# A cross-attention and gated-FFN layer: a pair's full-array products gathered in two of its four macros, half of the output projection one pair later, and VectorE's order changed with them

## The chip, the cores and the metric

The kernel runs on one core of one Trainium2 chip. The metric is device time in microseconds (us) of one execution. TensorE (PE) does the matrix products, VectorE (DVE) and ScalarE (ACT) the elementwise work, GpSimd (POOL) splits tiles and weights into high and low parts, and SyncE (SP) issues nearly all DMAs.

## The reference, cut to what matters

```python
B, Q, S, D, HEADS, DH = 4, 512, 1024, 256, 16, 64
lat = layer_norm(layernorm(x), g, b);  ctx = layer_norm(ctx_1024, g, b)
q = heads(lat @ Wq);  k, v = heads(split(ctx @ Wkv))
k = rope(k, cos, sin)
attn = softmax(clip(q @ k.T / 8, -11, 11));  x = x + (attn @ v) @ Wo + bo
t = layernorm(x)                               # then 16 experts, hidden 128, D 256
x = x + sum_e(relu(t @ keys[e]) * sigmoid(t @ sel[e])) @ values[e])
```

The clip is applied after the exponential, by its limits e^-11 and e^11, which is the same. All large products except attn @ v take operands that are split in a high and a low part and are the sum of three products (high·high, high·low, low·high).

## The kernel before, in words

The attention works on 32 pairs (4 batches of 8 pairs of heads, 128 columns). Each engine has a function `iteration(n)` that emits its work on pair n in an order written out by hand; nothing is scheduled by a tool, and engines meet only in semaphores. A pair has 8 steps of 128 context rows, two to a macro, so four macros m = 0 to 3.

On PE a macro is three blocks:

- **scores**: `scores(n, s)` for two steps, q times k of two heads in the two halves of the array's rows (in the trace `64*128`, source line L846);
- **full-array products** (`128*128`, L147 from the helper `product`): what the next pairs need;
- **attend**: `attend(n, s)` for the two steps of the macro before, probabilities times v of two heads in the two halves of the array's columns (`128*64`, L859). Macro 0 attends the last two steps of pair n-1 and ends with `denominators(n - 1)` (`128*32`, L872), the column sums of the summed probabilities.

The full-array products of pair n are, before the change: in macro 0 k of pair p = n+1 (`project_k`, two halves, into job_ps0 and job_ps1); in macro 1 q of pair p (`q_product`, job_ps0), the first half of v for a later pair (`project_v(n, 0)`, job_ps1), and the first half of the output projection of pair n-2 (`project_y(..., mt=0)`, into side_ps); in macro 2 the transposes of one context tile (`turn_tile`, pairs 0 to 21; every second one, with x rows, has four instead of two) and the second half of the output projection; in macro 3 the second half of v (job_ps0, after `q_split`). Pairs 30 and 31 have no v to make.

ACT does `exp` of two steps per macro, rounds q and k to their high parts (`round_q`, `round_k`), copies k, v, the attended output and the denominators out of PSUM (`evac_k`, `store_v`, `evac_o`), and applies the layer norm's affine part to a turned tile. DVE does per pair: `clip` of eight steps, four `sum_up` (two steps' probabilities added), two `sum_quad` (denominators wait for both), `rope_times` (two products), `rope_add`, `split_q`, `split_k`, two `add_y`, `scale_o`, `split_o`, `invert_den`, and `stats` and `normalize` of a tile. POOL computes the tile's reciprocal deviation (`rstd`), splits it (`split_tile`), and in pairs 0 to 5 also splits weights (`split_weights`, `split_v_weights`).

SP's queue per pair, in this order: four DMAs of `swap_k(p)` (rows of k swapped for the rope, after `evac_k`), the next context tile, `turn_den(n-1)`, `store_inv(n-1)`, `spread_inv(n-1)`, and from pair 5 on `fetch_pack(n+3)`, two DMAs of 384 KB with split weights, which wait until both halves of the output projection of pair n-2 are done (the pack's buffer holds that pair's Wo).

Buffers that order the work: two score banks, so `scores(n, s)` waits for `exp` of step s-2; four probability buffers, so `exp` of step s waits for `attend` and `sum_up` of step s-4; job_ps0 and job_ps1 for k, q, v and tiles; side_ps for both halves of the output projection and the denominators, each after the last reader's `add_y` or copy. `evac_o(n-1)` waits for `split_o(n-2)`.

## Time and profile before

| | us |
|---|---|
| median of 3 runs (1039.69 to 1040.93) | 1039.74 |
| the profiled execution, its own time | 1040.09 |
| its span, first to last instruction | 1037.9 |
| PE busy | 987.5 (95%) |
| DVE busy | 821.8 (79%) |
| ACT busy | 514.9 (50%) |
| POOL busy | 256.5 (25%) |

The attention runs from about 49 to 837 us of the span, the experts after it. In the attention PE executes almost without a gap. A busy PE is not a PE at its peak: the start of each matmul matters, since matmuls overlap in the pipeline, so the rows below are to be read by the distance from one start to the next.

### The profile page before, as it was taken

What the parts mean: (1) busy time and instruction counts of PE and PEld (TensorE: products, weight loads), DVE (VectorE), ACT (ScalarE), POOL (GpSimd) and SP (SyncE); (2) the same over time, 40 slices, a digit from 0 to 9 for tenths busy, and PEclk for the clock granted to TensorE, in tenths of its full rate; (3) what the DMA queues carried; (4) which work ended last, traced back from release to release, by engine and by line L of the source; (5) the groups of instructions that cost most, each with busy time, mean ns of one, the idle gap of its engine ahead of it and who ended that gap; (6) DMA issues with size and microseconds to landing.
All of it is one profiled execution on the core that took longest, in us unless ns stands there. A gap on an engine that the chain in (4) does not pass through costs nothing. (4 is left out here: it accounts for less than half of the span.)

```text
span 1037.9 us, 15273 instructions
## 1 busy us (share of the span) xinstructions
PE 987.5 (95%) x5336; PEld 605.9 (58%) x5336; DVE 821.8 (79%) x1239; ACT 514.9 (50%) x759; POOL 256.5 (25%) x241
## 2 busy tenths in 40 slices
PE   4599999999999999999999999999999889999998
PEld 3455555555555555555555555555555358888886
DVE  5499999888989999999999978998889876545422
ACT  5465555555555555655555555555555442222221
POOL 5442423211111111211111100321000135545442
PEclk9799999999999999999999999999999899999999
DMA  6344333332323232322222233222222471332321
GB/s 172 114 143 126 100 93 106 100 93 68 92 67 93 71 102 89 97 87 73 87 72 88 71 93 83 82 82 82 82 62 64 130 256 53 122 123 101 123 82 41
DMA packets 68952, 100.34 MB, mean 97 GB/s; under 512 B 21968, under 2 KB 44752, under 8 KB 66832
## 3 DMA queue, kind: packets, MB, share of 16 engines
q1 hardware_dynamic: 68880, 99.41, 31.7%
q8 instruction: 41, 0.67, 0.3%
q14 instruction: 31, 0.25, 0.1%
HBM read 70.01 MB, written 10.75 MB: 78 GB/s over the span
## 5 line engine op out<-in xcount | busy, mean ns | idle before, releaser
L1033 ACT ACTIVATE wide_a<-score_ps 128x1024 f32<-128x1024 f32 x256 | 249.2, 1029 | 149.1 <-PE score_ps L846 149.1
L1239 DVE TENSOR_SCALAR wide_a<-wide_a 128x1024 f32<-128x1024 f32 x256 | 181.5, 740 | 74.9 <-ACT wide_a L1033 74.8
L1248 DVE TENSOR_TENSOR p_sum<-wide_a 128x1024 f32<-128x1024 f32 x128 | 161.7, 1263 | 2.3
L859 PE MATMUL o_ps<-wide_a,values_a 128*64 128x512 f32 x512 | 124.0, 605 | 0.0
L859 PE MATMUL o_ps<-wide_a,v_sb 128*64 128x512 f32 x512 | 124.0, 605 | 0.0
L846 PE MATMUL score_ps<-q_hi,k_hi 64*128 64x512 f32 x512 | 115.6, 448 | 0.8 <-DVE k_lo L1218 0.8
L1781 DVE SCALAR_TENSOR_TENSOR act<-h_ps,wide_a 128x512 f32<-128x512 f32 x64 | 44.2, 690 | 90.0 <-PE h_ps L147 88.2
L846 PEld LDWEIGHTS score_ps<-q_hi,k_hi 64*128 64x128 f32 x512 | 48.4, 185 | 111.9 <-issue 99.6
L1552 POOL TENSOR_TENSOR act_lo<-act,act_hi 128x512 fp32r<-128x512 f32 x64 | 84.8, 1324 | 96.5 <-ACT act_hi L1698 96.5
L1698 ACT CAST act_hi<-act 128x512 fp32r<-128x512 f32 x64 | 39.7, 621 | 135.4 <-DVE act L1781 135.4
L846 PE MATMUL score_ps<-q_hi,k_lo 64*128 64x512 f32 x512 | 102.0, 394 | 0.0
L846 PE MATMUL score_ps<-q_lo,k_hi 64*128 64x512 f32 x512 | 101.8, 393 | 0.0
L649 POOL CAST wide_hi<-ctx_t 128x256 fp32r<-128x256 f32 x22 | 23.9, 1088 | 241.3 <-ACT x_t L986 123.2
L1254 DVE TENSOR_TENSOR p_sum<-p_sum 128x1024 f32<-128x1024 f32 x64 | 78.3, 1224 | 0.0
L634 POOL TENSOR_TENSOR rstd_sb<-var_sb,power 128x2 f32<-128x2 f32 x32 | 30.7, 958 | 180.6 <-DVE var_sb L1172 101.2
L1040 ACT COPY o_raw<-o_ps 128x512 f32<-128x512 f32 x32 | 18.8, 587 | 107.1 <-DVE o_lo L211 105.8
L147 PE MATMUL job_ps<-wv_hi,wide_hi 128*128 128x256 f32 x240 | 70.8, 295 | 0.0
L147 PE MATMUL job_ps<-wv_hi,wide_lo 128*128 128x256 f32 x240 | 67.7, 282 | 0.0
L147 PE MATMUL job_ps<-wv_lo,wide_hi 128*128 128x256 f32 x240 | 67.5, 281 | 0.0
L859 PEld LDWEIGHTS o_ps<-wide_a,v_sb 128*64 128x64 f32 x512 | 31.0, 136 | 57.4 <-issue 47.9
L859 PEld LDWEIGHTS o_ps<-wide_a,values_a 128*64 128x64 f32 x512 | 31.0, 136 | 55.3 <-issue 45.8
L147 PE MATMUL job_ps<-wide_hi,w_hi 128*128 128x512 f32 x128 | 55.2, 431 | 5.1 <-POOL wide_lo L639 2.8
(203 smaller groups left out, 2006.5 us busy)
## 6 DMA issues: line engine op xcount, KB each, us to landing
wide_a<-sel_dram SPq DMA_DIRECT2D x16, 1024.0 KB, 4.6
k_swap<-k SPq DMA_DIRECT2D x124, 128.0 KB, 2.3
w_hi<-packs_hi SPq DMA_DIRECT2D x26, 384.0 KB, 3.9
w_lo<-packs_lo SPq DMA_DIRECT2D x26, 384.0 KB, 4.4
den<-inv_dram SPq DMA_DIRECT2D x64, 128.0 KB, 2.9
ctx_raw<-ctx SPq DMA_DIRECT2D x24, 128.0 KB, 2.3
packs_hi<-w_hi SPq DMA_DIRECT2D x8, 384.0 KB, 3.3
packs_lo<-w_lo SPq DMA_DIRECT2D x8, 384.0 KB, 3.6
```

What stands on the lines that cost most here:

```text
L147: mm = pe.matmul(out, lhsT, rhs, start=start and i == 0, stop=stop and i == len(terms) - 1)
L634: pool.tensor_tensor(rstd_sb[slot][:], var_sb[slot][:], power[:], ALU.pow).then_inc(rstd_ready, 1)
L649: pool.tensor_copy(ctx_at(ctxT_hi, t), ctx_t32[:]).then_inc(tile_hi, 1)
L846: mm = pe.matmul(score_ps[s % 2][:, h, :], k[par][rows, s * P:(s + 1) * P], q[par][rows, :], start=(i == 0), stop=(i == len(terms) - 1))
L859: mm = pe.matmul(o_ps[DH * h:DH * h + DH, :], v_sb[n // 2 % 2][:, at:at + DH], probs[s % RING][:, h, :], start=(s == 0), stop=(s == STEPS ...
L1033: act.activation(probs[s % RING][:], score_ps[s % 2][:], ACT.Exp, scale=DH ** -0.5).then_inc(exp_done, 1)
L1239: dve.tensor_scalar(probs[s % RING][:], probs[s % RING][:], CLIP_HI, CLIP_LO, ALU.min, ALU.max).then_inc(clipped, 1)
L1248: dve.tensor_tensor(p_sum[m][:], first, second, ALU.add).then_inc(summed_up, 1)
L1254: dve.tensor_tensor(second[:], first[:], second[:], ALU.add).then_inc(quads_up, 1)
L1552: pool.tensor_tensor(act_lo[e % ARING][:], act32[e % ARING][:], act_hi[e % ARING][:], ALU.subtract).then_inc(act_split, 1)
L1698: act.copy(act_hi[e % ARING][:], act32[e % ARING][:]).then_inc(act_hi_done, 1)
L1781: dve.scalar_tensor_tensor(out=act32[e % ARING][:], in0=h_ps[e % ARING][:], scalar=0.0, in1=gates[:, at:at + 512], op0=ALU.max, op1=ALU.mu ...
```

## The change

PE's full-array products of macros 1 and 3 go to macro 2, and the second half of the output projection goes one pair on, to macro 0. Macros 1 and 3 are then scores and attend alone (in the last pair the second half for pair 29 stays in macro 3). The order of DVE and ACT follows.

```diff
 # PE
                     scores(n, 2 * m)
                     scores(n, 2 * m + 1)
+                    if m == 0 and n >= 3:
+                        pe.wait_ge(y_added, 2 * (n - 3) + 1)
+                        project_y(pe, sh, n - 3, 1, side_ps, w_hi[n % 2], w_lo[n % 2], (n - 1) % 2)
                     if m == 0 and p < NPAIR:
                         project_k(p, 0)
                         project_k(p, 1)
-                    if m == 1 and p < NPAIR:
+                    if m == 2 and p < NPAIR:
                         pe.wait_ge(k_evac, 2 * p + 1)
                         q_product(p)
-                    if m == 1 and n + 2 < NPAIR:
+                    if m == 2 and n + 2 < NPAIR:
                         project_v(n, 0)
+                    if m == 2 and n >= 2:
+                        pe.wait_ge(den_evac, n)
+                        pack_ready(n - 2 + WO_LAG)
+                        project_y(pe, sh, n - 2, 0, side_ps, w_hi[p % 2], w_lo[p % 2], n % 2)
+                    if m == 2 and n + 2 < NPAIR:
+                        project_v(n, 1)
                     if m == 2 and t < TILES:
...
-                    if m == 3 and n + 2 < NPAIR:
-                        project_v(n, 1)
-                    if n >= 2 and m in (1, 2):
...
+                    if m == 3 and n == NPAIR - 1:
+                        pe.wait_ge(y_added, 2 * (n - 2) + 1)
+                        project_y(pe, sh, n - 2, 1, side_ps, w_hi[p % 2], w_lo[p % 2], n % 2)
 # ACT
-                    if m == 1:
+                    if m == 2:
                         if p < NPAIR:
                             round_q(p)
                         if n + 2 < NPAIR:
                             store_v(j, FILLS + 2 * n)
-                    if m == 2:
                         if p < NPAIR:
                             round_k(p)
+                        if n + 2 < NPAIR:
+                            store_v(j, FILLS + 2 * n + 1)
...
                     if m == 3:
-                        if n + 2 < NPAIR:
-                            store_v(j, FILLS + 2 * n + 1)
 # DVE
                 for m in range(MACROS):
-                    if m == 2 and p < NPAIR:
-                        rope_add(p)
-                    if m == 3 and n >= 2:
+                    last = n == NPAIR - 1
+                    if m == 1 and t < TILES:
+                        dve.wait_ge(turned, t)
+                        normalize(t, ctx_n[:], x_n[:])
+                    if last and m == 3:
                         add_y(dve, sh, n - 2, 1, side_ps, bo)
...
+                    if m == 1 and p < NPAIR:
+                        rope_times(p)
                     clip(n, 2 * m + 1)
-                    if m == 1 and p < NPAIR:
-                        split_q(p)
                     if m == 0 and n > 0:
                         sum_quad(n - 1, 1)
+                    if m == 0 and n >= 3:
+                        add_y(dve, sh, n - 3, 1, side_ps, bo)
+                    if m == 2 and n >= 2:
+                        add_y(dve, sh, n - 2, 0, side_ps, bo)
                     sum_up(n, m)
...
                     if m == 1:
...
                         if n > 0:
                             invert_den(dve, sh, n - 1)
...
                         if p < NPAIR:
-                            rope_times(p)
+                            split_q(p)
+                            rope_add(p)
                     if m == 2:
...
                             split_k(p)
...
                         if n > 0 and not last:
                             scale_o(dve, sh, n - 1)
                         if not last:
                             sum_quad(n, 0)
```

On PE, around macro 3 of a middle pair: before, the twelve v products, of which the last five are shown, stand between the scores and attend.

```order
L147 MATMUL job_ps<-wv_lo,wide_hi 128x256
L147 MATMUL job_ps<-wv_hi,wide_lo 128x256
L147 MATMUL job_ps<-wv_hi,wide_hi 128x256
L147 MATMUL job_ps<-wv_lo,wide_hi 128x256
L147 MATMUL job_ps<-wv_hi,wide_lo 128x256
L859 MATMUL o_ps<-wide_a,v_sb 64x512 x4
```

After, macro 3's scores are followed by attend, then by the scores of the next pair's macro 0, then by the second half of the output projection (side_ps) and the first products of k (wide_hi, w_hi).

```order
L846 MATMUL score_ps<-q_lo,k_hi 128x512 x2
L859 MATMUL o_ps<-wide_a,v_sb 64x512 x4
L846 MATMUL score_ps<-q_hi,k_hi 128x512 x2
L846 MATMUL score_ps<-q_hi,k_lo 128x512 x2
L846 MATMUL score_ps<-q_lo,k_hi 128x512 x2
L846 MATMUL score_ps<-q_hi,k_hi 128x512 x2
L846 MATMUL score_ps<-q_hi,k_lo 128x512 x2
L846 MATMUL score_ps<-q_lo,k_hi 128x512 x2
L147 MATMUL side_ps<-o_hi,w_hi 128x512
L147 MATMUL side_ps<-o_lo,w_hi 128x512
L147 MATMUL side_ps<-o_hi,w_lo 128x512
L147 MATMUL job_ps<-wide_hi,w_hi 128x512
```

The scores and attend of macros 1 and 3 now touch, and the v products stand in macro 2.

On DVE, macro 1 of a pair without x rows, before: both clips (wide_a), `split_q` (q_lo), `sum_up`, `normalize` (ctx_n), `invert_den`, `add_y`, `rope_times` (k, k_swap), then `rope_add`.

```order
L1239 TENSOR_SCALAR wide_a<-wide_a 128x1024 x2
L1202 TENSOR_TENSOR q_lo<-job_ps,q_hi 128x512
L1248 TENSOR_TENSOR p_sum<-wide_a 128x1024
L1182 TENSOR_SCALAR ctx_n<-ctx_raw,mv_c,rstd_sb 128x256
L175 TENSOR_TENSOR inv_rows<-den_rows 128x8
L177 RECIPROCAL inv_rows<-inv_rows 128x8
L223 TENSOR_TENSOR yT<-side_ps,yT 128x512
L1208 TENSOR_TENSOR k<-k,cos_sb 128x1024
L1209 TENSOR_TENSOR k_swap<-k_swap,sin_sb 128x1024
L1213 TENSOR_TENSOR k<-k,k_swap 128x1024
```

After, the same macro, to the first clips of macro 2:

```order
L1184 TENSOR_SCALAR ctx_n<-ctx_raw,mv_c,rstd_sb 128x256
L1241 TENSOR_SCALAR wide_a<-wide_a 128x1024
L1210 TENSOR_TENSOR k<-k,cos_sb 128x1024
L1211 TENSOR_TENSOR k_swap<-k_swap,sin_sb 128x1024
L1241 TENSOR_SCALAR wide_a<-wide_a 128x1024
L1250 TENSOR_TENSOR p_sum<-wide_a 128x1024
L175 TENSOR_TENSOR inv_rows<-den_rows 128x8
L177 RECIPROCAL inv_rows<-inv_rows 128x8
L1204 TENSOR_TENSOR q_lo<-job_ps,q_hi 128x512
L1215 TENSOR_TENSOR k<-k,k_swap 128x1024
L1241 TENSOR_SCALAR wide_a<-wide_a 128x1024 x2
```

`normalize` has moved ahead of the clips and the rope's products between them; `split_q` has moved behind `invert_den`, where it waits for the q product of PE's macro 2.

## Rows read from the trace of the kernel before

**Rows 1.** Busy time by stage: us, PE, PEld, DVE, ACT, POOL, PEclk, DMA share, GB/s
```profile
49.00:809.00 760.00, 749.86 (x4255) 422.45 (x4256) 677.95 (x939) 426.22 (x598) 138.22 (x127) 1.00 0.31 90
```

**Rows 2.** Timeline of PE, pair 14 from macro 1's products on: start, length, work
```profile
402.58 0.50 PE L147 MATMUL job_ps<-xT_hi,w_hi 128*128 128x512 f32 x1
...
406.30 1.94 PE L859 MATMUL o_ps<-wide_a,v_sb 128*64 128x512 f32 x8
408.16 0.50 PE L846 MATMUL score_ps<-q_hi,k_hi 64*128 64x512 f32 x2
...
414.18 0.39 PE L846 MATMUL score_ps<-q_lo,k_hi 64*128 64x512 f32 x2
414.50 0.39 PE L147 MATMUL job_ps<-wv_hi,wide_hi 128*128 128x256 f32 x1
414.72 0.28 PE L147 MATMUL job_ps<-wv_lo,wide_hi 128*128 128x256 f32 x1
...
416.11 1.94 PE L859 MATMUL o_ps<-wide_a,v_sb 128*64 128x512 f32 x8
417.97 0.50 PE L846 MATMUL score_ps<-q_hi,k_hi 64*128 64x512 f32 x2
```

**Rows 3.** Timeline of PE, macro 3 of pair 30, which has no full-array product
```profile
806.40 0.39 PE L846 MATMUL score_ps<-q_lo,k_hi 64*128 64x512 f32 x2
806.72 1.94 PE L859 MATMUL o_ps<-wide_a,v_sb 128*64 128x512 f32 x8
```

**Rows 4.** Timeline of PE, the denominators of pairs 0, 5, 16, 17, 29, 30 and 31
```profile
78.38 1.07 PE L872 MATMUL side_ps<-p_sum,ones 128*32 128x512 f32 x8 [0.75 <-DVE p_sum L1254]
...
203.74 1.06 PE L872 MATMUL side_ps<-p_sum,ones 128*32 128x512 f32 x8
...
473.57 1.06 PE L872 MATMUL side_ps<-p_sum,ones 128*32 128x512 f32 x8
...
497.78 1.06 PE L872 MATMUL side_ps<-p_sum,ones 128*32 128x512 f32 x8
...
794.03 1.06 PE L872 MATMUL side_ps<-p_sum,ones 128*32 128x512 f32 x8
...
815.96 1.93 PE L872 MATMUL side_ps<-p_sum,ones 128*32 128x512 f32 x8 [3.60 <-DVE p_sum L1254]
...
836.59 1.06 PE L872 MATMUL side_ps<-p_sum,ones 128*32 128x512 f32 x8 [1.44 <-DVE p_sum L1254]
```

**Rows 5.** Timeline of ACT, macros 1 and 2 of the pair of rows 2
```profile
405.27 0.62 ACT L1012 CAST q_hi<-job_ps 128x512 fp32r<-128x512 f32 x1
...
409.17 1.94 ACT L1033 ACTIVATE wide_a<-score_ps 128x1024 f32<-128x1024 f32 x2 [2.78 <-PE score_ps L846]
```

**Rows 6.** Timeline of DVE, the same pair
```profile
406.06 0.68 DVE L1202 TENSOR_TENSOR q_lo<-job_ps,q_hi 128x512 fp32r<-128x512 f32 x1
...
409.32 1.22 DVE L1208 TENSOR_TENSOR k<-k,cos_sb 128x1024 f32<-128x1024 f32 x1
410.45 1.22 DVE L1209 TENSOR_TENSOR k_swap<-k_swap,sin_sb 128x1024 f32<-128x1024 f32 x1
...
412.85 1.29 DVE L1239 TENSOR_SCALAR wide_a<-wide_a 128x1024 f32<-128x1024 f32 x2
...
417.05 1.82 DVE L1239 TENSOR_SCALAR wide_a<-wide_a 128x1024 f32<-128x1024 f32 x2
```

**Rows 7.** Timeline of DVE, `normalize` in pair 0
```profile
60.16 1.91 DVE L1182 TENSOR_SCALAR ctx_n<-ctx_raw,mv_c,rstd_sb 128x256 f32<-128x256 f32 x1
```

**Rows 8.** Timeline of POOL, `split_weights` in pair 0
```profile
59.24 2.68 POOL L670 TENSOR_TENSOR w_lo<-w_raw,w_hi 128x768 fp32r<-128x768 f32 x1
```

**Rows 9.** Timeline of SP's queue, four issues of `swap_k`
```profile
423.27 2.46 SPq L516 DMA_DIRECT2D k_swap<-k  x4
```

**Rows 10.** The page, DMA issues: count, KB each, median us to landing
```profile
k_swap<-k SPq DMA_DIRECT2D x124, 128.0 KB, 2.3
w_lo<-packs_lo SPq DMA_DIRECT2D x26, 384.0 KB, 4.4
```

More of the change, by code:

```diff
@@ L947, in iteration @@
                             logits(pe, sh, job_ps[1], lambda k: xT_hi[:, 0, k, :], lambda k: xT_lo[:, 0, k, :])
-                    if m == 3 and n + 2 < NPAIR:
-                        project_v(n, 1)
-                    if n >= 2 and m in (1, 2):
-                        if m == 1:
-                            pe.wait_ge(den_evac, n)
-                            pack_ready(n - 2 + WO_LAG)
-                        else:
-                            pe.wait_ge(y_added, 2 * (n - 2) + 1)
-                        project_y(pe, sh, n - 2, m - 1, side_ps, w_hi[p % 2], w_lo[p % 2], n % 2)
+                    if m == 3 and n == NPAIR - 1:
+                        pe.wait_ge(y_added, 2 * (n - 2) + 1)
+                        project_y(pe, sh, n - 2, 1, side_ps, w_hi[p % 2], w_lo[p % 2], n % 2)
                     if m > 0:
@@ L1112, in iteration @@
                             evac_o(n - 1)
-                    if m == 1:
+                    if m == 2:
                         if p < NPAIR:
@@ L1325, in iteration @@
                 for m in range(MACROS):
-                    if m == 2 and p < NPAIR:
-                        rope_add(p)
-                    if m == 3 and n >= 2:
+                    last = n == NPAIR - 1
[3 more added lines that the diff above has]
+                    if last and m == 3:
                         add_y(dve, sh, n - 2, 1, side_ps, bo)
-                    last = n == NPAIR - 1
-                    if last and m == 3:
                         split_keys(3)
@@ L1349, in iteration @@
                     if m == 1:
-                        if t < TILES:
-                            dve.wait_ge(turned, t)
-                            normalize(t, ctx_n[:], x_n[:])
                         if n > 0:
                             invert_den(dve, sh, n - 1)
-                        if n >= 2:
-                            add_y(dve, sh, n - 2, 0, side_ps, bo)
                         if p < NPAIR:
-                            rope_times(p)
+                            split_q(p)
+                            rope_add(p)
                     if m == 2:
@@ L1363, in iteration @@
                             split_k(p)
-                        if n == 29:
-                            invert_gate(dve, sh, 0, 1)
-                    if m == 3:
                         if n > 0 and not last:
@@ L1370, in iteration @@
                             sum_quad(n, 0)
+                        if n == 29:
+                            invert_gate(dve, sh, 0, 1)
+                    if m == 3:
                         if n == 23:
```

## The prediction, made before the changed kernel had run

> **What bounds the kernel now.** I read the stage table first. From 49 to 809 us of the span PE is busy for 749.9 of 760 us at the full clock, 2.4 GHz; DVE is busy for 678 us, 89%, so it is the second bound and its order matters [rows 1]. Then the timeline of PE, by starts. Attend runs eight passes in 408.16 - 406.30 = 1.86 us, so a slot of 512 columns takes 0.2325 us [rows 2]. The full-array products of macro 1 are nine slots of 512 and twelve of half that, 15 slots or 3.49 us, and take 3.72; those of macro 3 are six slots' worth, 1.395 us, and take 416.11 - 414.50 = 1.61 [rows 2]. So a visit to the full array costs 0.23 and 0.21 us beside its work. One can see where: the first product's slot is 0.22 in place of 0.116 (414.50 to 414.72), the rest is in the last slot before attend. Entering from the scores costs 0.32 - 0.23 = 0.09 (414.18 to 414.50), but scores that go straight to attend pay the same 0.32 [rows 2, 3], so that part stays.
>
> Third, the starts of the denominators, one per pair. Pair 17's is 24.21 us after pair 16's, a pair in which PE waits for nothing [rows 4]. The 24 pairs to number 29 take 794.03 - 203.74 = 590.3 us against 24 x 24.21 = 581.0; some 4 us of the 9.3 are transposes and logits that pair 17 has not (estimated from the slots), so 5 us are waits. The five to number 5 take 125.4 against 5 x 24.21 - 1.4 (pair 1 has no output projection, six slots) = 119.7: over 5 us are waits. Pair 0 has about 2 more. At the end come 3.60 and 1.44 us of waiting for `sum_quad`, and after the first of them PE runs at its lower level, 1.2 GHz: the same denominators take 1.93 instead of 1.06 [rows 4].
>
> **The change, part by part.**
>
> *Two visits less per pair.* No product is added or removed. Macros 1 and 3 lose their visit, 0.21 + 0.23 = 0.44 us, which I take as 0.42 since v's second half and the moved y product may keep a few hundredths where they join. The moved work falls into visits that exist. Pairs 0 to 29 gain this, 12.6 us; pair 30 gains one visit, and pair 31 has one more (the product for pair 28 in macro 0). Sum: -12.5 us. A direct look at a pair whose macros 1 and 3 are bare exists only at the end [rows 3].
>
> The Trainium skill, "TensorEngine Tiling (Array Packing)", Key Properties, says that changing the tiling mode drains TensorE. By that rule each change of form costs, scores to attend as well. Counting changes, a pair has 13 before and 11 after; the rows put 0.09 at the end of the scores whichever form follows, and more at both ends of a full-array visit, so the sum goes by the visit.
>
> *DVE's new chain to `split_q`.* This is the one place where PE newly waits in the middle of its work: `project_v(n, 1)` waits for `q_split` in the same macro, with tile transposes and attend queued behind it. From macro 2's start PE wants it after scores 1.6, q 1.5, v 1.4, y 0.7 = 5.2 us. The q product ends at 1.6 + 1.5 + 0.2; the cast is 0.62 [rows 5] and `split_q` 0.68 [rows 6], so it is ready at 4.6: a margin of 0.6 us, if DVE is free at 3.9. DVE's chain there starts with the exp of macro 1. The exps end 1.0 and 1.0 us apart, the first about 2.0 us after the scores' start (409.17 is 1.0 after 408.16, the pair of them 1.94) [rows 2, 5], or 2.3 if ACT first has to copy the output of the last pair. Then come clip 0.6, two rope products 2.3, clip 0.6, a sum 1.15 and the inverses 0.3: 4.95 [rows 6]. That is 7.0 to 7.3 after macro 1's start. Macro 1 is now 1.6 + 1.86 = 3.46 long, so DVE is free 3.5 to 3.8 us into macro 2, just before q's high part is there. In a middle pair PE loses nothing; behind this DVE has work until `sum_quad`, which now ends about 4.7 us into macro 0, against 7.1 where the denominators want it (scores 1.6, y 0.7, k 3.0, attend 1.86). So the waits of the middle pairs go, and those for head rows too, since `sum_up` of macro 3 no longer has `scale_o` and a `sum_quad` between it and them. Of the 5 us I leave 1.3 for pairs with x rows, where POOL's splits lengthen DVE's clips (1.82 in place of 1.29) [rows 6]: -3.7 us.
>
> *Pairs 0 to 5.* Here POOL splits weights just while DVE is in that chain. In pair 0 `normalize` took 1.91 us and ended at 62.07, right after POOL's 2.68 us split that ended at 61.92 [rows 7, 8]. Before, this lay in macro 1 with the whole pair to make it good. Now one such block (some 1.5 us) is 0.9 more than the margin of 0.6, so 0.9 us in pairs 1, 3, 4 and 5, and about 2.5 in pairs 0 and 2, where v weights are split as well: 8.6 us. They take the place of 7.3 us of waits: +1.3 us. The bounds: if POOL's splits fall beside ACT-bound moments, 3 us of waits remain (-4); if each is met twice, 12 (+5). The value is nearest to the one block that the row shows.
>
> The Trainium skill, "SBUF — State Buffer", "Who interferes with whom", says the pair of ports that DVE and GpSimd share is held for a whole instruction, by whoever issues first. The trace agrees: 1.91 us for an instruction that ends 0.15 after POOL's. A price that only shared the port between them would leave this term smaller; the sum goes by the row.
>
> *The end.* Pair 31's scores find the k split done sooner, `sum_quad` of pair 30 has less before it, and 0.9 us of its wait is filled by the moved y product. I work out a wait of 1.6 us there in place of 3.60, and of about 1 in place of 1.44. Whether PE falls to 1.2 GHz decides the rest: the slow stretch costs 0.87 in the denominators alone and as much again in the scores behind [rows 4]. I take -3.5 us; 0 and -5.5 are the ends.
>
> *DMAs.* `fetch_pack(n+3)` waits for both halves of y of pair n-2. The second is now 2.6 us into macro 0 of the next pair, 3.4 us ahead of `swap_k` on the same queue, and lands 4.4 us after its issue [rows 10]. The pack is needed a pair later; that is hidden. But the rope's products now start 10.8 us after macro 0's start, in the middle of macro 1 and not behind all else in it. The four swaps take 2.46 us to issue and the last lands 2.3 after its issue [rows 9, 10]: issued from 6.0, done by 10.2. Cover 0.6 us, cost 0 if the fetch is out of the way by then. It was spread over the same engines at some 160 GB/s (2 x 384 KB in about 4.9 us), gone at about 8.3.
>
> Sum: -12.5 - 3.7 + 1.3 - 3.5 = -18.4 us. The profiled execution took 1040.09 us (2.2 outside its span), so 1021.7; the median lies 0.35 below it: 1021.3 us.
>
> **The rivals.**
>
> *B, DVE becomes the bound.* If `split_q` is ready 1 us later than worked out, in every pair, PE waits 0.4 us before the second v half: 12 us back, 1033 us. For it: DVE's 89% over a pair that gets shorter by 0.42, a margin of 0.6. Against: DVE's own idle time of two us in macro 1, which the new order places in the same chain as needed waits, and not all of it is needed.
>
> *C, slower: the swaps fall behind the fetch.* Were the four swaps (512 KB) queued wholly behind the fetch, at its 160 GB/s they would need 3.3 us from 9.0 on and land at 12.3, not 10.2. The rope's products, then the clip, the sum and `split_q` queued behind them on DVE, and v on PE would be late by 2.1 - 0.6 - 0.6 = 0.9 us in each of 26 pairs: +23 us, 1045 us. It turns the sign when the last swap lands 1.9 us late, at 4.2 us instead of 2.3. Against it: most of the fetch has landed before the first swap is issued.
>
> *D, the gain of the visits isn't there.* If the extra slots belong to the products and reappear (a first slot of 0.32 for attend after bare scores, or at the join), only waits move: 1021 + 12.5 = 1034 us. Against it stands the start of attend at 806.72 [rows 3], with no longer slot than after products.
>
> **How the numbers follow.** The forecast 0.62; B 0.18; C 0.11; D 0.09. The forecast's own range is 1013 (early waits nearly gone, the end at its best) to 1029. To hold 8 in 10 the range goes up over B and D and stops short of C: 1012 to 1036. About 0.2%, 2 us, can be told from no change. B and D are nearly always faster; so faster 0.85, within 0.2% 0.05, slower 0.10.
>
> **What would show it.** Right: in middle pairs, denominators 23.8 us apart; attend 0.32 after the last score pass and 3.46 us from macro 1's start to macro 2's; no wait for `sum_quad` before them; waits of PE for `q_lo` about 1 us each in pairs 0 to 5 and none later; no PE at 1.2 GHz in pair 31. Wrong: a wait for `q_lo` in every pair (B), with `k_swap` as what DVE waited for (C), or visits of more than 0.25 us beside their work (D).

## The result, and the profile after

| | before | after |
|---|---|---|
| median, us | 1039.74 (1039.69 to 1040.93) | 1034.95 (1033.66 to 1035.25) |
| ratio | | 0.9946, 95% interval 0.9931 to 0.9960 |
| the profiled execution, us | 1040.09 | 1033.66 |
| its span, us | 1037.9 | 1031.4 |

The change gives 4.8 us by the medians and 6.4 in the profiled executions. The sign was forecast, the size (18.4) was not. (Medians here and below are of fast runs: one run of e7 took 1380.31 us at a granted clock of 0.66, one of the kernel before 3162.86 us, and neither is counted.) First the stage of [rows 1] again, in the kernel after (us, then busy time of PE, PEld, DVE, ACT, POOL, the granted clock, DMA share, GB/s):

```profile
49.00:809.00 760.00, 746.48 (x4270) 429.23 (x4266) 689.84 (x946) 436.94 (x601) 145.71 (x127) 0.99 0.31 89
```

PE is busy less than before, so it waits more, while DVE went from 678 to 690 us of the same stretch. DVE is what the new order leans on. The starts of the denominators, which answer to [rows 4] (pairs 0, 5, 16, 17, 29, 30, 31):

```profile
83.01 1.06 PE L872 MATMUL side_ps<-p_sum,ones 128*32 128x512 f32 x8
...
209.75 0.64 PE L872 MATMUL side_ps<-p_sum,ones 128*32 128x512 f32 x4
...
474.61 1.07 PE L872 MATMUL side_ps<-p_sum,ones 128*32 128x512 f32 x8
...
498.59 1.07 PE L872 MATMUL side_ps<-p_sum,ones 128*32 128x512 f32 x8
...
789.00 1.06 PE L872 MATMUL side_ps<-p_sum,ones 128*32 128x512 f32 x8
...
810.90 1.07 PE L872 MATMUL side_ps<-p_sum,ones 128*32 128x512 f32 x8 [2.80 <-DVE yT L223]
...
830.13 1.07 PE L872 MATMUL side_ps<-p_sum,ones 128*32 128x512 f32 x8 [1.44 <-DVE p_sum L1256]
```

These starts cut the span in three, and the thirds are the ledger of all that follows. Up to pair 5 the changed kernel **loses 6.0 us** (209.75 against 203.74), over pairs 6 to 29 it gains 11.0 (579.25 against 590.29), behind them 1.5 (the rest of the span, 242.4 against 243.9).

The middle is what the prediction described. Timeline of PE, macro 1 of pair 14 and, lower down, the end of macro 2 of pair 15, the kernel after (the answer to [rows 2]):

```profile
403.39 0.50 PE L846 MATMUL score_ps<-q_hi,k_hi 64*128 64x512 f32 x2
...
404.66 0.39 PE L846 MATMUL score_ps<-q_lo,k_hi 64*128 64x512 f32 x2
404.98 1.94 PE L859 MATMUL o_ps<-wide_a,v_sb 128*64 128x512 f32 x8
406.84 0.50 PE L846 MATMUL score_ps<-q_hi,k_hi 64*128 64x512 f32 x2
...
436.20 0.38 PE L147 MATMUL job_ps<-wv_hi,wide_hi 128*128 128x256 f32 x1
436.41 0.29 PE L147 MATMUL job_ps<-wv_lo,wide_hi 128*128 128x256 f32 x1
...
437.60 0.28 PE L147 MATMUL job_ps<-wv_hi,wide_lo 128*128 128x256 f32 x1
...
438.03 1.94 PE L859 MATMUL o_ps<-wide_a,v_sb 128*64 128x512 f32 x8
```

Macro 1 has no full-array work any more: 406.84 - 403.39 = 3.45 us, and attend starts 0.32 after the last score pass, both as forecast. In pair 15 the first product of v's second half holds its slot for 0.21 us (436.20 to 436.41) where the others of the same form take 0.12. In pair 14 that slot is 0.15. That this is `q_lo`, ready only just then, e11 shows below. Tile transposes now stand before attend, and from the last product (437.60) to attend are 0.43 us, 0.12 of it that product, 0.31 the transposes.

The start is what it did not describe. Pair 0, timelines of POOL, of DVE and of PE:

```profile
57.12 0.19 POOL L666 TENSOR_TENSOR carry_pool<-power 128x2 f32<-128x2 f32 x1
...
58.35 2.37 POOL L670 TENSOR_TENSOR w_lo<-w_raw,w_hi 128x768 fp32r<-128x768 f32 x1
60.69 1.18 POOL L678 TENSOR_TENSOR carry_pool<-power 128x2 f32<-128x2 f32 x1
61.81 1.61 POOL L679 CAST wv_hi<-wv_raw 128x512 fp32r<-128x512 f32 x1
63.49 1.59 POOL L681 TENSOR_TENSOR wv_lo<-wv_raw,wv_hi 128x512 fp32r<-128x512 f32 x1
```

```profile
58.94 2.87 DVE L1210 TENSOR_TENSOR k<-k,cos_sb 128x1024 f32<-128x1024 f32 x1
61.73 1.21 DVE L1211 TENSOR_TENSOR k_swap<-k_swap,sin_sb 128x1024 f32<-128x1024 f32 x1
62.87 1.09 DVE L1241 TENSOR_SCALAR wide_a<-wide_a 128x1024 f32<-128x1024 f32 x1
63.99 2.17 DVE L1250 TENSOR_TENSOR p_sum<-wide_a 128x1024 f32<-128x1024 f32 x1
66.09 0.68 DVE L1204 TENSOR_TENSOR q_lo<-job_ps,q_hi 128x512 fp32r<-128x512 f32 x1
```

```profile
66.82 0.58 PE L147 MATMUL job_ps<-wv_hi,wide_hi 128*128 128x256 f32 x1 [4.99 <-DVE q_lo L1204]
```

The first rope product takes 2.87 us, not 1.22 [rows 6]; it ends 1.09 after POOL's `w_lo` (61.81 against 60.72), so it did nothing until POOL was through. `sum_up` does the same behind `wv_lo` (ends at 66.16, 1.08 after 65.08). PE waits 4.99 us for `q_lo`, and then has lost its clock as well (a stretch of the same view as the first row above):

```profile
66.80:72.00 5.20, 5.18 (x20) 3.92 (x22) 5.17 (x6) 2.99 (x6) 0.00 (x0) 0.50 0.27 85
```

From 66.8 to 72.0 PE runs at 1.2 GHz. The same happens in pair 2, behind a wait of only 2.22 us: from 120.04 on the transposes and attend run at 1.2 GHz (granted clock 0.50 from 120 to 122), and attend takes 2.93 us from start to start in place of 1.87.

```profile
118.40 0.39 PE L147 MATMUL job_ps<-wv_hi,wide_hi 128*128 128x256 f32 x1 [2.22 <-DVE q_lo L1204]
...
121.03 3.01 PE L859 MATMUL o_ps<-wide_a,v_sb 128*64 128x512 f32 x8
```

In pairs 0 to 5 it waits 10.2 us in all for `q_lo`:

```profile
PE job_ps L147 <- DVE q_lo L1204: 10.2, 6, 5.0
```

### The profile page after: what moved, and what is told of

Its sections match the earlier page's. It is cut to its first block and busy times, and to the rows that moved or that the text cites. A ratio compares the mean times of both kernels' runs of the same rounds, so it can differ in the third digit from the quotient of the medians.

```text
span 1031.4 us, 15273 instructions
## 1 busy us (share of the span) xinstructions
PE 978.8 (95%) x5336; PEld 610.5 (59%) x5336; DVE 826.5 (80%) x1239; ACT 523.5 (51%) x759; POOL 263.4 (26%) x241
## 5 line engine op out<-in xcount | busy, mean ns | idle before, releaser
L1241 DVE TENSOR_SCALAR wide_a<-wide_a 128x1024 f32<-128x1024 f32 x256 | 186.0, 754 | 47.6 <-ACT wide_a L1036 47.3
L1250 DVE TENSOR_TENSOR p_sum<-wide_a 128x1024 f32<-128x1024 f32 x128 | 159.3, 1244 | 2.3
L649 POOL CAST wide_hi<-ctx_t 128x256 fp32r<-128x256 f32 x22 | 27.2, 1238 | 228.7 <-ACT x_t L989 115.5
L1256 DVE TENSOR_TENSOR p_sum<-p_sum 128x1024 f32<-128x1024 f32 x64 | 80.6, 1260 | 0.0
L147 PE MATMUL job_ps<-wv_hi,wide_hi 128*128 128x256 f32 x240 | 70.1, 292 | 10.2 <-DVE q_lo L1204 10.2
L1009 ACT COPY k<-job_ps 128x512 f32<-128x512 f32 x64 | 37.5, 587 | 46.0 <-PE job_ps L147 46.0
```

Source lines behind the costliest of these rows:

```text
L147: mm = pe.matmul(out, lhsT, rhs, start=start and i == 0, stop=stop and i == len(terms) - 1)
L1009: act.copy(k_half(k32, half), job_ps[half][:]).then_inc(k_evac, 1)
L1241: dve.tensor_scalar(probs[s % RING][:], probs[s % RING][:], CLIP_HI, CLIP_LO, ALU.min, ALU.max).then_inc(clipped, 1)
L1250: dve.tensor_tensor(p_sum[m][:], first, second, ALU.add).then_inc(summed_up, 1)
L1256: dve.tensor_tensor(second[:], first[:], second[:], ALU.add).then_inc(quads_up, 1)
```

## The experiments

Each was timed beside the kernel before, whose median was 1040.1 to 1040.9 us there against 1039.74 beside the kernel after; so a microsecond between medians of two rows of the table says little. "Start" is pair 5's denominators, "middle" from there to pair 29's, "end" the rest of the span, all in us from the rows of each trace:

| run | median | ratio to before | start | middle | end |
|---|---|---|---|---|---|
| before | 1039.74 | | 203.7 | 590.3 | 243.9 |
| after | 1034.95 | 0.9946 | 209.8 | 579.3 | 242.4 |
| e1 splits late | 1036.39 | 0.9959 (0.9945 to 0.9973) | 209.9 | 583.4 | 242.3 |
| e2 no weight split | 1023.96 | 0.9845 (0.9831 to 0.9858) | 198.1 | 580.0 | 242.6 |
| e3 the same, before | 1033.96 | 0.9933 (0.9920 to 0.9947) | 198.6 | 589.8 | 243.3 |
| e4 y alone, before | 1048.92 | 1.0073 (1.0055 to 1.0090) | 207.3 | 595.4 | 244.1 |
| e5 v back | 1040.14 | 0.9998 (0.9989 to 1.0007) | 206.5 | 588.1 | 243.3 |
| e7 tail | 1040.63 | 1.0001 (0.9988 to 1.0014) | 209.9 | 580.8 | 245.8 |
| e8 q_lo first | 1034.17 | 0.9936 (0.9917 to 0.9955) | 207.7 | 580.9 | 242.2 |
| e9 weights to ACT, DVE | 1029.34 | 0.9885 (0.9867 to 0.9903) | 204.2 | 581.1 | 242.7 |
| e10 scaling late | 1047.66 | 1.0066 (1.0052 to 1.0080) | 212.1 | 591.5 | 243.0 |
| e11 q_lo first, odd pairs | 1053.02 | 1.0124 (1.0108 to 1.0139) | 211.6 | 595.1 | 243.2 |
| e12 e9, v early | 1028.61 | 0.9884 (0.9869 to 0.9899) | 202.9 | 581.6 | 242.0 |
| e13 e12, more order | 1028.96 | 0.9888 (0.9873 to 0.9903) | 201.7 | 582.3 | 244.7 |
| e14 e12, o_lo early | 1025.71 | 0.9861 (0.9846 to 0.9876) | 199.2 | 580.8 | 242.7 |
| e15 e14, sums early | 1026.80 | 0.9866 (0.9851 to 0.9881) | 201.1 | 582.2 | 242.0 |
| e16 order alone | 1031.65 | 0.9913 (0.9898 to 0.9928) | 206.2 | 582.6 | 243.4 |

The three columns are from one execution of each kernel, and it need not be the median one: that of e16 took 1034.42 us, that of e7 1038.77. "Middle" also moves where nothing was edited. The edits of e1, e2, e8, e9 and e12 to e16 end by pair 7 and e7's is in the last pair, yet their middles are 0.8 to 4.2 us longer than after's, and 0.4 to 3.0 us of this lies in pairs 22 to 28. No run here explains it.

### GpSimd's weight splits

**e2 and e3: cut the splits of pairs 0 to 5 to 8 columns**, in the kernel after and in the one before.

```diff
-pool.tensor_tensor(w_lo[par][:], w_raw[:, 0:WC], w_hi[par][:], ALU.subtract)
+pool.tensor_tensor(w_lo[par][:, 0:8], w_raw[:, 0:8], w_hi[par][:, 0:8], ALU.subtract)
```

(w_hi, wv_hi and wv_lo likewise.)

> The changed kernel, with GpSimd's splits of the weights in pairs 0 to 5 cut to 8 columns each (w_hi, w_lo, wv_hi, wv_lo are left unfilled beyond them; the rest is whole). Theory P: these splits hold the SBUF port while VectorE is in the chain that ends in split_q, and that is why pairs 0 to 5 became 6 us slower instead of faster. Then the wait for q_lo in pair 0 (5 us) falls under 1 us, TensorE does not drop to 1.2 GHz there, and the denominators of pair 5 start 7 to 9 us earlier than in the changed kernel (209.75): about 1027 us in all. Rival O (order): the chain on VectorE is too long by itself, with the rope between the clips, and the weights' splits only lie beside it; then pair 0 still waits 3 us or more and the kernel stays at 1032 to 1034 us.

> The kernel before, with the same splits of weights cut to 8 columns. It tells how much of the waits in pairs 0 to 5 of the kernel before came from the port. Theory P: some 5 us (the waits for sum_quad and x_n there), 1035 us, less than the changed kernel gains from the same cut, because before the change nothing on TensorE waited for VectorE in the middle of that chain. Rival O: the cut is worth the same to both kernels, 1 to 3 us.

Theory P was right both times, though it forecast too little for the kernel after: that one gets 11.0 us faster (1034.95 to 1023.96), the one before only 5.8 by the medians (1039.74 to 1033.96). The difference stands in the start: 11.7 against 5.1. So POOL's splits cost both kernels DVE's time, and the new order could bear it less. Without them the whole change is worth 10.0 us. PE keeps its clock in pair 0 now. What is left of the wait there, 1.9 us and not under 1, is no matter of POOL's weight splits:

```profile
65.40 0.39 PE L147 MATMUL job_ps<-wv_hi,wide_hi 128*128 128x256 f32 x1 [1.90 <-DVE q_lo L1204]
```

In pairs 0 and 1 no output projection stands between the halves of v, so 0.7 us less covers the chain to `q_lo`. That is not the whole of it: in e2 pair 1 does not wait, and in pair 0 DVE's chain starts late.

**e1: let the splits wait for `q_lo`.**

```diff
+pool.wait_ge(q_split, n + 2)
 split_weights(n + 2)
```

(SP's load of the weights goes behind its transfers of the denominators.)

> The changed kernel whole, but in pairs 0 to 5 GpSimd waits for q_split before it splits weights, so that its splits lie behind VectorE's chain; on SyncE's queue the load of the next weights moves behind store_inv and spread_inv, so that these do not wait for the split. Theory P: as good as leaving the splits out, less what they cost later beside clips and sums: pair 5's denominators 6 to 8 us earlier, 1027 to 1028 us. Rival O: no gain, 1033 to 1035 us, or slower, since the weights are ready later.

Theory P missed by 8 us; rival O's "or slower" came, but not for its reason. The waits for `q_lo` fell from 10.2 to 1.7 us, but the start kept its length. The longest waits of PE from 56 to 210 us:

```profile
PE o_ps L860 <- issue: 3.2, 4, 1.1
PE side_ps L873 <- DVE yT L221: 2.7, 1, 2.7
PE side_ps L873 <- DVE yT L223: 2.4, 3, 1.3
PE job_ps L147 <- DVE q_lo L1205: 1.7, 1, 1.7
```

Moved by some 6 us, the splits hit the chain to the denominators. My expectation priced one victim; this place was no quieter for DVE than the first.

**e9: take the splits off POOL**: ACT rounds in macro 1, DVE subtracts at the start of macro 3.

```diff
-split_weights(n + 2)            # POOL, pairs 0 to 5
+round_weights(w)                # ACT, behind the exps of macro 1
+split_weights(n + 2)            # DVE, ahead of the clips of macro 3
```

(SP's load of the weights is moved as in e1.)

> The kernel after, with the weights' splits of pairs 0 to 5 taken off GpSimd: ScalarE rounds (w_hi, wv_hi) in macro 1, VectorE subtracts (w_lo, wv_lo) at the start of macro 3, and SyncE's load of the next weights goes behind the transfers of the denominators. All work is done. Theory P (VectorE stands still while GpSimd's instructions of two operands run): VectorE gets 6 x .93 + 2 x .63 = 6.8 us of work and loses the stretches of 1.0 to 1.7 us in its multiplications and sums (cutting the splits out altogether gave 11 us); 1025 to 1029. Rival B (VectorE's own work is what is too much in pairs 0 to 5): the 6.8 us come on top, 1034 to 1040. Rival K (k of the next pair waits for w_lo, or the weights' load comes too late): waits of k's products in macro 0 of pairs 1 to 6, 1032 or more.

As theory P said, at its upper edge: 5.6 us less than after, though DVE does more work of its own (6.8 us by the expectation's estimate). `w_lo` takes 0.95 us on DVE; on POOL it took 2.37 in pair 0 and held up a product for 1.65.

```profile
147.57 0.95 DVE L1201 TENSOR_TENSOR w_lo<-w_raw,w_hi 128x768 fp32r<-128x768 f32 x1
```

### The order of VectorE

**e8: in pairs 0 to 5 write `q_lo` before the second clip.**

```diff
 rope_times(p)
+split_q(p)                      # pairs 0 to 5; taken out behind sum_up
 clip(n, 2 * m + 1)
```

> The kernel after, with one edit in pairs 0 to 5: VectorE writes q_lo ahead of the second clip and the sum of macro 1 instead of behind them. Theory O (it is the order: q_lo, on which the second half of v waits, stands behind 3.3 us of work that nobody needs yet, stretched by GpSimd's weight splits): the wait of v falls from 5.0 to about 2 us in pair 0, by 1 us or more in the others, and TensorE's clock stays at 2.4 GHz: 6 to 8 us, 1028. Rival B (VectorE has no room left in pairs 0 to 5 while GpSimd splits the weights): the waits for q_lo go and come back as waits for clips, sums and the scaled output at the next scores and attend, 1034 to 1036.

Rival B: 1034.17, within the error of the 1034.95 without it. Pair 0's `v` block fell from 9.3 to 4.9 us, and the waits for `q_lo` from 10.2 to 1.7; in their place came waits for `yT`, for `sum_quad`, and at attend of macro 1, the first behind the denominators. (Some expectations call it attend of macro 0, after the block of VectorE's program that it waits for.)

**e10: undo one part of DVE's order**, `scale_o` and `sum_quad(n, 0)` back to the start of macro 3.

```diff
-if m == 2: ... split_k(p); scale_o(n - 1); sum_quad(n, 0)
+if m == 3: scale_o(n - 1); sum_quad(n, 0); ...
```

> The kernel after, with one part of VectorE's new order undone: the scaling of the output and the first sum_quad stand in macro 3 again, ahead of its clips, not at the end of macro 2. Theory W (these 2 us of VectorE's work were what the denominators waited for, 0.2 to 0.4 us in every pair with x rows and more in pairs 0 to 5): attend before the denominators gets longer again, 0.2 to 0.8 us a pair in 12 to 30 pairs: 1039 to 1048. Rival S (the earlier start of macro 0's chain comes from the shorter PE side, the order matters little): 1035 to 1036.

The size is theory W's: 12.7 us slower than after, and slower than before. The place is not: the denominators hardly waited; attend of macro 1 did, and in pairs 24 to 26 the second half of v (1.9 us for `q_lo`), the denominators (1.4) and once k (2.1). See it in pair 12, timelines of ACT and PE:

```profile
360.70 0.59 ACT L1043 COPY o_raw<-o_ps 128x512 f32<-128x512 f32 x1 [3.26 <-DVE o_lo L211]
```

```profile
360.87 0.40 PE L846 MATMUL score_ps<-q_lo,k_hi 64*128 64x512 f32 x2
361.38 1.94 PE L859 MATMUL o_ps<-wide_a,values_a 128*64 128x512 f32 x8
```

Attend may write `o_ps` only once ACT has copied it out, and ACT may overwrite `o_raw` only once DVE has taken `o_lo` from it. Attend starts 0.51 after the last score pass, not 0.32 [rows 3]. This chain, in neither my prediction nor my first expectations, is the one by which DVE's lateness reaches PE in macro 1 here. (After's copy in macro 1 meets no such wait: attend follows 0.32 after the scores.)

**e11: `q_lo` before the second clip in the odd pairs**, against the 0.1 us at the join of y and v.

> The kernel after, with one edit in the odd pairs (those that turn no x rows): VectorE writes q_lo ahead of the second clip and the sum of macro 1. Theory J (the second half of v starts there with a product of 0.23 us instead of 0.12, since q_lo comes 0.1 us too late): v's second half takes 1.42 instead of 1.52 in every odd pair, an odd pair 23.86 instead of 23.96: -1 us in pairs 7 to 29, and up to -1 more in the early ones: 1033 to 1034. Rival Q (the first product after the output projection costs that in these pairs whatever VectorE does, or VectorE now waits for q_hi with the clip behind it): 23.96 or longer, 1035 or more.

Rival Q, and far beyond it: 18 us slower than after, for an edit that moves one instruction of 0.65 us. The join did shrink, v's second half took 1.42 us. Timelines of DVE, ACT and PE in pair 11:

```profile
344.92 0.69 DVE L1204 TENSOR_TENSOR q_lo<-job_ps,q_hi 128x512 fp32r<-128x512 f32 x1 [1.44 <-ACT q_hi L1015]
```

```profile
338.48 0.59 ACT L1043 COPY o_raw<-o_ps 128x512 f32<-128x512 f32 x1 [3.41 <-DVE o_lo L211]
```

```profile
338.48 0.43 PE L846 MATMUL score_ps<-q_lo,k_hi 64*128 64x512 f32 x2
339.17 1.94 PE L859 MATMUL o_ps<-wide_a,v_sb 128*64 128x512 f32 x8 [0.26 <-issue]
```

DVE now stands still for 1.44 us waiting for `q_hi`, and two pairs together take 49.7 us where they took 48.1: all of it comes back as waits of PE (1.0 us at attend of macro 1, 0.5 before the denominators). So DVE has no room for this even in the middle pairs: busy for 690 of 760 us, it could not stand still for 1.44 us of 48 without PE waiting.

**e4: in the kernel before, only y's second half one pair later.**

```diff
+if m == 0 and n >= 3: project_y(n - 3, 1)      # PE, ahead of k
+if m == 0 and n >= 3: add_y(n - 3, 1)          # DVE, behind sum_quad(n - 1, 1)
-if m == 2: project_y(n - 2, 1)
```

> The kernel before, with one part of the change: only the second half of the output projection (and VectorE's addition to it) goes to macro 0 one pair later, beside k's products; q, v and the first half stay where they were. Theory V (a pair pays .4 to .5 us per stretch of full-array products that lies between scores and attend, and nothing per group inside such a stretch): macro 2 keeps its stretch wherever tiles are turned (pairs 2 to 21) and loses it only in pairs 22 to 30, so 9 x .2 to .4 us: 1036 to 1038, middle pairs with a tile unchanged within .1 us. Rival G (each group of full-array products has its own price, .2 us, wherever it stands): nothing is gained anywhere, 1040. Rival W (one half of the work that macro 2 waited for was the sum on VectorE before it): all pairs from 3 on get .1 to .2 us shorter, 1034 to 1036.

All three expectations missed: 9 us slower. DVE's addition now stands between `sum_quad` and PE's denominators, with DVE's old order too late for it:

```profile
282.73 1.06 PE L872 MATMUL side_ps<-p_sum,ones 128*32 128x512 f32 x8 [1.08 <-DVE yT L223]
```

With e10 this shows that the moves on PE and VectorE's order are no sum of parts: one of PE's moves without the new order, and all of them without one part of it, are each slower than doing nothing.

### The stretches of full-array work

**e5: v's second half and its copy back in macro 3.**

```diff
-if m == 2 and n + 2 < NPAIR: project_v(n, 1)
+if m == 3 and n + 2 < NPAIR: project_v(n, 1)
```

> The changed kernel with the second half of v (and its copy) back in macro 3, so that a visit to the full array returns to each of 30 pairs and nothing waits for q_split within macro 2. By the price of a visit, 0.21 us, it loses 6.3 us in 30 pairs; it gets back the waits for q_lo, about 10 us and the slow clock in pair 0: 1029 to 1032 us, middle pairs 0.2 us longer (24.3 and 24.2 in place of 24.13 and 23.96). If visits cost nothing in themselves, the middle pairs keep their length and it takes about 1024 us.

Missed. Of the early waits 3.3 us came back, not the most of them (the wait for `q_lo` went, waits at attend of macro 1 took its place). The middle got 8.9 us longer, 24.57 and 24.35 a pair in place of 24.12 and 23.96. That is 0.42 for the one stretch restored, more than the 0.21 of the prediction, because there the transposes wait some 0.24 for ACT's copy of v's first half (it ends at 265.97), which v's second half otherwise covers. Less this wait, the stretch itself costs about 0.2 us. Timeline of PE, a middle pair of e5 (between products of y the starts are 0.23 apart, before the transposes 0.48):

```profile
265.41 0.39 PE L147 MATMUL side_ps<-o_lo,w_hi 128*128 128x512 f32 x1
265.64 0.40 PE L147 MATMUL side_ps<-o_hi,w_lo 128*128 128x512 f32 x1
266.12 0.41 PE L762 MATMUL job_ps<-ident,ctx_n 128*128 128x128 f32 x2
```

### Pairs 0 and 1, and the path to o_lo

**e12: e9, and v's second half in macro 3 in pairs 0 and 1 only.**

> GpSimd's weight splits taken over by ScalarE (high parts) and VectorE (low parts) as in the earlier run, and beside it the second half of v back in macro 3 in pairs 0 and 1 alone, where no output projection stands between it and q. Theory C (in pairs 0 and 1 the wait for q_lo, 2.7 and 0.2 us, is the chain q, rounding, subtraction itself, which nothing covers there): saves 2.7 + 0.2 less 0.4 for each visit that comes back, 2.1 us: 1027. Rival B (VectorE is behind in pair 0 by its own work, and the wait comes back at the scores or the denominators): 1029 to 1030.

1028.61 against 1029.34: the medians differ by less than the runs scatter, so neither theory C nor rival B is decided by the time. The start is 1.3 us shorter: the wait of 1.7 us for `q_lo` is gone, but 0.85 us came back before the denominators of pair 0, as rival B had it, and 1.5 us at the transposes of pairs 0 and 1, which now wait for ACT's copy of v.

**e13: e12, sums and y addition early in macro 0 of pairs 1 to 6, the last key split behind the last `sum_quad`.**

> The run with the weights on ScalarE and VectorE and v early in pairs 0 and 1, and two more changes of VectorE's order: in pairs 1 to 6 the sum_quad of the pair before goes ahead of the first clip of macro 0 and the addition of the moved y half between the two clips; in the last pair the split of the last keys goes behind the last sum_quad. Theory V (in pairs 2 to 6 the denominators wait 0.3 to 1 us for yT, written last in VectorE's chain clip, clip, sum_quad, addition; and the last denominators wait behind 1.2 us of key split that nobody needs yet): -2 in pairs 2 to 6 and -1.2 at the end: 1024. Rival L (VectorE has that much to do whatever the order, and the clips, which attend waits for, come late instead): no gain, 1027 or the same as the run beside it.

No gain. The denominators' waits went in pairs 2 to 6 and those at attend of macro 1 grew from some 0.7 to 1.0 us and more. At the end the last two blocks of attend took 5.95 us in place of 7.43: the wait for the clips fell from 1.77 to 0.29, that for the last `sum_quad` stayed 1.44. PE ran at 1.2 GHz there twice, behind pair 30's denominators and again behind pair 31's:

```profile
805.50:811.10 5.60, 5.60 (x28) 2.44 (x28) 2.58 (x4) 3.46 (x5) 0.00 (x0) 0.70 1.01 313
826.70:833.20 6.50, 5.44 (x14) 3.78 (x13) 2.00 (x4) 1.46 (x2) 0.10 (x1) 0.50 0.56 210
```

The first costs 1.55 us, and even so pair 31's denominators come 0.4 us sooner after pair 30's than in e12. The loss lies behind them: 3.1 us, the moved key split (`o_lo` waits for it, and the last output projection for `o_lo`, 0.76) and the second stretch. The kernel after, in the first place and after the same wait (2.80 us against 2.82), kept its clock (1.00 from 810.9 to 816.5).

**e14: e12, and `o_lo` written early in macro 0 (pairs 2 to 7).**

```diff
+if m == 0 and 2 <= n < 8: split_o(n - 2)       # ahead of sum_up and stats
 sum_up(n, m)
```

> The kernel with the weights' splits on ScalarE and VectorE and v early in pairs 0 and 1, and one more edit: in pairs 2 to 7 VectorE writes o_lo ahead of the sum and the statistics of macro 0, not behind them. Theory O (attend in macro 0 waits .5 to .8 us there since ScalarE may copy the output only after o_lo is written, and VectorE writes that 2.2 us late, behind work nobody needs yet): scores of macro 0 take 1.6 again in pairs 2 to 6 instead of 2.2 to 2.4, 5 x .7 = 3.5 us less, 1025. Rival L (VectorE has that much work in these pairs, the wait moves to the denominators or to q_lo): 1028 to 1029.

Theory O: the start is 3.7 us shorter, the scores of macro 1 take 1.6 us again. Pair 3 without (e12) and with the edit, ACT's copy and PE's attend:

```profile
130.91 0.59 ACT L1039 COPY o_raw<-o_ps 128x512 f32<-128x512 f32 x1 [4.62 <-DVE o_lo L211]
```

```profile
131.60 1.94 PE L855 MATMUL o_ps<-wide_a,v_sb 128*64 128x512 f32 x8 [0.50 <-issue]
```

```profile
126.99 0.59 ACT L1039 COPY o_raw<-o_ps 128x512 f32<-128x512 f32 x1 [2.10 <-DVE o_lo L211]
```

```profile
128.70 0.40 PE L842 MATMUL score_ps<-q_lo,k_hi 64*128 64x512 f32 x2
129.04 1.94 PE L855 MATMUL o_ps<-wide_a,v_sb 128*64 128x512 f32 x8
```

The time is the 1025 of theory O. This is the fastest kernel here that does all the work: 1025.71 us, 9.2 less than after, 1.4% less than before.

**e15: the same with e13's early sums.**

> The same, and sum_quad and the moved y addition early too (ahead of the first clip, and between the clips, pairs 1 to 6), the edit that took the wait from the denominators and gave it to attend in the run of everything. Theory O: with o_lo early as well neither the denominators nor attend wait in pairs 2 to 6, 24.1 us each: 1024. Rival L: the wait comes back once more (q_lo, the clips), 1028.

Not better (1026.80; the start 1.9 us longer): waits for `q_lo` of 0.3 to 0.7 us came back in each pair from 2 to 7. Rival L's mechanism, at a third of its price.

**e16: the order alone**, e8's, e13's and e14's edits of pairs 0 to 7 on the kernel after, POOL's splits in place.

> The kernel after with VectorE's order alone changed in the early pairs: q_lo ahead of the second clip (pairs 0 to 5), sum_quad, moved y addition and o_lo early in macro 0 (pairs 1 to 7); GpSimd still splits the weights. Theory O (what VectorE is late with is a matter of order): the early waits go, 1027 to 1029. Theory P (GpSimd's weight splits cost VectorE time it does not have, whatever the order): at most the clock's share comes back, 1031 to 1035.

Theory P: 3.3 us by the medians (the five runs lie between 1029.62 and 1034.42). With the splits off POOL, order and v's second half early in pairs 0 and 1 gave as much on top (e9 to e14, 3.6). Both are needed, the splits are the larger (5.6).

### The end

**e7: the inversion of pair 30's denominators behind the third sum of the last pair.**

```diff
-if m == 1: ... invert_den(n - 1)
+if last and m == 2: invert_den(n - 1)          # behind sum_up
```

> The kernel after, with one edit in the last pair: VectorE takes the inversion of the denominators of pair 30 behind the third sum of the last pair instead of behind the second. Theory D (the inversion waits 1.8 us for a transfer that SyncE issues behind the loads of the experts' values, and everything that VectorE has queued behind it, clips and sums included, is late, which TensorE then waits for in the last pair): the wait of 3.7 us in attend of pair 31 falls to about 2, the time to 1033. Rival L (the inversion is itself on the path, since pair 30 is scaled and projected behind it): the wait only moves, 1035 to 1036.

Slower than after by 3.4 us of "end", though DVE's wait for `den_rows` was avoided. Most of the 3.4 is the clock: PE ran at 1.2 GHz behind the denominators of pair 30 and again behind those of pair 31, 1.6 and 1.3 us longer than in e12, which kept its clock there. The edit itself gave nothing, as rival L said: the wait moved. The inverses now reach `scale_o` late, which waits 1.42 us for another transfer with the last clip queued behind it, and the last two blocks of attend take 8.6 us in place of 7.4. And a clip moved into the time of POOL's key split and stood still for it (timelines of POOL and DVE):

```profile
818.74 3.22 POOL L701 TENSOR_TENSOR wide_lo<-k_swap,wide_hi 128x1024 fp32r<-128x1024 f32 x1 [106.01 <-ACT wide_hi L1101]
```

```profile
820.52 2.59 DVE L1241 TENSOR_SCALAR wide_a<-wide_a 128x1024 f32<-128x1024 f32 x2 [0.81 <-ACT wide_a L1036]
...
830.01 0.69 DVE L198 TENSOR_TENSOR o_raw<-o_raw,den 128x512 f32<-128x512 f32 x1 [1.42 <-DMA den<-inv_dram]
```

## Why the prediction was wrong

By its own four terms, each against what the starts of the denominators show (the visits of pairs 0 to 5 are taken at the price that the middle pairs show, so their sum with the third row is measured and the division between the two is not):

| term | forecast | measured |
|---|---|---|
| visits, 30 pairs | -12.5 | -8.4 |
| waits of the middle pairs | -3.7 | -4.3 |
| pairs 0 to 5 beside the visits | +1.3 | +7.7 |
| the end | -3.5 | -1.5 |
| sum | -18.4 | -6.5 |

**The step that failed most is "Pairs 0 to 5": "one such block (some 1.5 us) is 0.9 more than the margin of 0.6"** (0.9 us in pairs 1, 3, 4 and 5, 2.5 in 0 and 2, up to 12 us at the outer bound). It holds 6.4 of the 11.9 us missed. By size: PE waited 10.2 us for `q_lo` where 8.6 were forecast; running at 1.2 GHz behind the waits of pairs 0 and 2 cost some 4 us, a term that the prediction does not have for these pairs; and the waits that these replaced were 5 to 6 us (5.2 in the trace of the kernel before, 5.1 given back by e3), not 7.3. So the clock is the largest part. The mechanism of the wait was named rightly; four things made it larger. The block was met more than once in the chain: 1.65 us in the rope product and 0.95 in the sum of pair 0. The margin of 0.6 was worked out with a y product of 0.7 between the halves of v, which pairs 0 and 1 do not have; in pair 0 the chain alone is 1.9 us late (e2). The wait of 5 us in pair 0 and that of 2.2 us in pair 2 cost PE its clock: against the same blocks in e2, 2.4 us in pair 0 (v slots of 0.21 for 0.12, attend 2.59 for 1.87, both from the starts) and 1.6 in pair 2. And the step priced only the chain to `q_lo`, while e1, e8 and e16 show that in these pairs a wait taken away there comes back, in whole or for the most part, at the denominators, attend or the clips.

The Trainium skill's "SBUF — State Buffer", "Who interferes with whom", says that whoever of DVE and GpSimd holds the shared port pair holds it for the whole instruction. The trace agrees: 1.09 us from POOL's end to DVE's end in the first rope product, 1.08 in the sum, both begun after POOL's instruction.

**Visits.** The stretches did go. But a pair in which neither kernel waits went from 24.21 to 23.96, and one with x rows, less the 0.22 wait that it lost, from 24.43 to 24.12: 0.25 and 0.31, not 0.42. Two things were overlooked. Transposes at the head of a stretch take 0.20 us for two and at its tail, before attend, 0.31; before the change they opened one. And in pairs without x rows the join with v pays 0.1 us for `q_lo`. "A margin of 0.6" was in truth a little under nothing, as the slot of 0.21 shows, which e11 brings back to 0.12.

**Middle waits.** The size is about right, and the waits for `sum_quad` went, as forecast. That the new order does it is shown by e10, which undoes part of it and loses 12.2 us in these pairs. But it loses them mainly through `o_lo` and ACT's copy, a chain that the prediction does not name, so that the size came out is partly luck.

**The end.** PE kept its clock, as forecast, but the waits hardly shrank: 2.80 for 3.60 where 1.6 was forecast (the last addition to `yT`, not `sum_quad`, decides there now), 1.44 for 1.44 where 1 was, and a new one of 1.77 in the last attend. On DVE two things stand ahead of the clip that it waits for: a wait for a transfer and the last key split. e13 takes the key split away, keeps the transfer, and has 0.29 of the 1.77 left; so the key split is what can be moved, while e7, which went for the transfer, gained nothing.

```profile
819.28 0.47 DVE L175 TENSOR_TENSOR inv_rows<-den_rows 128x8 f32<-128x8 f32 x1 [1.80 <-DMA den_rows<-den]
```

**The rivals.** B gave nearly the right time (1033) by luck: its wait for `q_lo` in every pair is 0.1 us, not 0.4. What it says of DVE, that it becomes the bound, is what e10 and e11 bear out. The measured time also lies within 1012 to 1036 only because that range was widened over B and D; the forecast's own ended at 1029. C did not come: DVE waited for `k_swap` 1.9 us in all over pairs 6 to 29. D's first slot of 0.32 for attend after bare scores is refuted by the 0.32 from the last score pass to attend, no more than before; but some 0.1 us a pair did come back, at the transposes. The 89% of DVE should have weighed more: that is how I read e10 and e11.

What stays open: why the same wait of 2.8 us in pair 30 costs the clock in some traces (e2, e4, e5, e7, e9, e10, e11, e13, e14, e16) and not in others (after, e1, e8, e12, e15). "End" is 242.0 to 242.4 us in these and 242.6 to 245.8 in those, so differences of that size are not explained by the edits. With one trace of each kernel, it can as well differ from execution to execution of the same kernel. Open too is why pairs 22 to 28 differ between kernels that are alike there. That POOL's smaller tile splits cost pairs 6 to 21 time is likely by the same mechanism but was not tried.

## What to carry to other kernels

An engine that sits between two others and is busy most of a stage (here VectorE, 89%) may have no slack where it counts: before moving its work, list each chain that leaves it (here `q_lo`, `sum_quad`, `yT`, `o_lo`) with what waits at its end, and price a delay on all of them, not on the one the change names. Price the clock as well: two waits for one tile cost some 4 us beyond themselves. Elementwise work on GpSimd is not free beside VectorE; 22 of its instructions (five lines of the program, in six pairs) cost this kernel 11 us, and giving them to ScalarE and to VectorE itself was cheaper than leaving them. Full-array products grouped together saved 0.25 to 0.31 us a pair for two stretches avoided, about 0.15 each, and only if what then stands last in the stretch does not pay at the other end.

## What the runs showed of the hardware

- Between DVE and POOL either can wait for the other. POOL's operation on two elements takes 0.19 us alone (57.12) and 1.18 us (60.69) beside DVE's rope product, which it had made wait.
- Whichever began first ran at its usual length, with POOL's rounding copies too. In pair 0 DVE's second product began at 61.73 and took its usual 1.21 us; POOL's copy to `wv_hi`, begun at 61.81, took 1.61 where it takes 0.61 in the kernel before (at 62.06), and the clip behind the product took 1.09 in place of 0.69. In pair 2 it is the same, and the next product, begun under the copy, took 1.63.
- PE went to 1.2 GHz behind 5 us of idling in pair 0 and behind 2.2 us of it in pair 2; behind 2.8 us in pair 30 it did so in ten traces of fifteen.
